# A graph-attention kernel's last layer: the barrier between projection and attention taken out, and its first attention step made beside the last projection rounds

## The chip, the cores and the metric

The kernel runs on one core of a Trainium2 chip. The metric is the device time of one execution in microseconds (us); the median of three runs of the kernel before is 1928.7 us (1923.83 to 1929.61). Everything below that has a moment in it ("at 1560.74") counts from the start of the profiled execution's span.

## The reference, cut to what matters

Two graph networks follow each other on 1250 nodes with 768 features and 40000 edges. The change is in the last convolution of the second one (in the kernel: layer DD), a relational graph attention with three edge types and one head:

```python
h = jax.nn.elu(h)                       # output of the convolution before
xr = jnp.einsum('nd,rdf->rnf', h, W)    # three projections, 768 x 768 each
alpha = jax.nn.leaky_relu((xr[etype, dst] @ q) + (xr[etype, src] @ k), 0.2)
m = segment_max(alpha, dst);  e = jnp.exp(alpha - m[dst])
z = segment_sum(e, dst);      a = e / (z[dst] + EPS)
out = segment_sum(a[:, :, None] * xr[etype, src], dst) + b
x = _layernorm(x + out)
```

## The kernel before, in words

**Dense form.** Nodes are padded to 1280, ten tiles of 128. Edges are counted into dense tables (`counts`, one per edge type), so attention is a dense product: for every pair of a source tile and a target tile, weights `counts * exp(...)` times projected rows. The last layer does both its projection and its attention with seven block products in place of eight (a Strassen scheme of 2 x 2 blocks: the names P1 to P7 and the sums `s1`..`s4`, `t1`..`t4`).

**Projection** (`project_d` on each engine). Six units (three types, two column halves) of five tile pairs make 30 rounds (`ROUNDS`). In a round TensorE (PE) makes seven products of 192 columns into PSUM (L1202), ScalarE (ACT) copies three of them (`keep_a`, `keep_b`, `keep_c`, L1563) and a fourth block (`fetch_c21`, L1585), VectorE (DVE) adds the rest up (`c22` L2096, `c11` L2087, `c12` L2109 to L2112), and ACT stores the round's five blocks to HBM (`store`, L1592, tensor `hs_d`). The products of two rounds are interleaved by the list `ORDER_D`; the semaphore `d_prod` counts them, and `DONE_D` is the count at which a given one is done. The last product of all is P3 of round 29. In between, DVE has searched the maxima, and from round 25 on the shift rows `pq` are turned, stored and fetched back to all partitions (`pq_rows_d`, L631, semaphore `pq_in`).

**Barrier.** Then every engine calls `end_phase`, which drains it and waits until all five have arrived. ACT comes to it only when all stores have landed:

```python
                store(ROUNDS - 1)
                for i in range(BLOCKS):
                    act.wait_ge(*d_blk_out[i].at(16 * ring_share(ROUNDS, i, BLOCKS)))
```

**Attention.** 75 steps: five groups `g` of two target tiles, and in each 15 pairs `m` of an edge type and a pair of source tiles. For step n, SyncE's queue (SP) loads projected rows `hs_d` (`h_load`, L796, 960 KB) into one of four places `h_slot`; DVE makes four quarters of exponents (`exponents_d`, L2367, in two instructions), ACT raises them (`exp_d`, L1788, two), DVE multiplies by the counts (`weights_d`, L2375, two) and makes six block sums (`sums_d`, L2385 to L2394; the fourth of them, L2390, is the first to read the loaded rows); PE multiplies (L1366, seven products of 384 or 385 columns). `d_ready` counts steps prepared, `d_used` steps multiplied. A load into a place, and exponents into one of four `a_slot`, wait until the step four before has been multiplied. The exponents of step n + 1 come ahead of the weights of step n.

All places of the attention (`a_slot`, `h_slot`) lie in `work`, over operands of the projection (`xT`, `xs`, `wsum`), and so can be written only when the projection is over. The order on SP after the barrier is load 0, load 1, the `pq` rows of type 1 (two transfers of 640 KB), loads 2, 3 and 4, the `pq` rows of type 2, loads 5 and on.

Of the kernel before, what the change touches and what calls it, by code (L numbers as in the profile page):

```python
# [29 lines left out]
P = 128  # L30
# [115 lines left out]
S_ROUND, MAX_ROUND, PQ_ROUND = 6, 8, 25  # L146
SAVE_AT = 1
# [9 lines left out]
def gnn_program(nc, t_in, out):  # L157
    with ExitStack() as ctx:
# [414 lines left out]
        def _(sp):  # L573
# [60 lines left out]
            def project_d(ci, s, ph):  # L634
# [26 lines left out]
                end_phase(sp, ph)  # L661

            def layer(ci, c, ph):
# [29 lines left out]
                if c is DD:  # L693
                    project_d(ci, s, ph)
# [96 lines left out]
                else:  # L791
                    def h_load(n):
# [3 lines left out]
                        sp.dma_start(h_slot[n % H_SLOTS][:, 0:5, 0:FH],  # L796
# [39 lines left out]
        def _(pool):  # L836
# [45 lines left out]
            for k in range(2, 6):  # L882
                end_phase(pool, k)
# [5 lines left out]
        def _(pe):  # L889
# [342 lines left out]
            def layer(ci, c, ph):  # L1232
# [74 lines left out]
                if c is DD:  # L1307
                    project_d(ci, s)
                    end_phase(pe, ph)
# [12 lines left out]
                pe.wait_ge(ones, 1 if c is A else ci)  # L1322
                if c is not DD:
                    body = c.unroll * c.R
# [23 lines left out]
                else:  # L1348

                    for g in range(TH):  # L1350
                        for m in range(STEPS_D):
                            n = g * STEPS_D + m
                            pe.wait_ge(d_ready, n + 1)
                            a, h = a_slot[n % A_SLOTS], h_slot[n % H_SLOTS]
                            for i, name in enumerate(PRODUCTS):
# [10 lines left out]
                                last = mm(bank(product_bank(g, i), width), a[:, at * P:(at + 1) * P], h[:, block_, 0:width],  # L1366
# [20 lines left out]
        def _(act):  # L1387
# [150 lines left out]

            def project_d(ci, s):
# [67 lines left out]
                for q in range(ROUNDS + 1):  # L1607
# [26 lines left out]
                    if q >= TH and q % TH == 0 and q // TH + 1 < len(UNITS):  # L1634
                        act.wait_ge(d_prod, DONE_D[q - 1, "P3"])
                        w_load(q // TH + 1)
                store(ROUNDS - 1)
                for i in range(BLOCKS):
                    act.wait_ge(*d_blk_out[i].at(16 * ring_share(ROUNDS, i, BLOCKS)))

            def layer(ci, c, ph):
# [122 lines left out]
                if c is DD:  # L1764
                    project_d(ci, s)
                    end_phase(act, ph)
# [11 lines left out]
                else:  # L1778
# [4 lines left out]
                    def exp_d(n):  # L1783
                        r, p = PAIRS_D[n % STEPS_D]
                        for q in range(2):
# [740 lines left out]
```

## Time and profile before

| what | value |
|---|---|
| median of 3 runs | 1928.7 us (1923.83 to 1929.61) |
| the profiled execution: its time, its span | 1925.18 us, 1923.3 us |
| granted TensorE clock, mean of the span | 0.973 |
| PE busy | 1777.4 us (92%) |
| DVE busy | 1549.1 us (81%) |
| ACT busy | 727.3 us (38%) |
| attention products of the last layer (L1366) | 341.1 us busy, 11.1 us idle before them |
| projection products of the last layer (L1202, the group that the page shows) | 98.1 us busy, 2.2 us idle before them |
| exponentials of the last attention (L1788) | 150 of them, 68.0 us busy, mean 500 ns |

Read it so: PE is the busiest engine over the span, but that is an average over stages. The idle time ahead of a line says how long the engine stood still just before instructions of that line, and what released it. Matmuls are pipelined and their ends are modelled, so their durations overlap; the distance between starts is the better measure of pace.

### The profile page before, as it was taken

The numbers are of one execution on the slowest core, as the hardware profiler recorded it, in microseconds if no ns is written. First come the engines' busy times: TensorE is split into PE (matmuls) and PEld (weight loads), VectorE is DVE, ScalarE is ACT, GpSimd is POOL, SyncE is SP. The second block draws the span as 40 slices with busy tenths as digits, with TensorE's granted clock in tenths as the row PEclk, the third lists the DMA queues.
The fourth block names the chain that finished last, engine by engine and source line by source line (L and its number), as shares of the span: only waits on it lengthen the run. The fifth ranks groups of instructions, "written<-read, shape, count | busy, mean of one in ns | idle before, by whom it ended". The sixth has DMA issues, their size and how long they took to land. (4 is left out here: it accounts for less than half of the span.)

```text
span 1923.3 us, 24256 instructions
## 1 busy us (share of the span) xinstructions
PE 1777.4 (92%) x8426; PEld 1334.4 (69%) x8427; DVE 1549.1 (81%) x2948; ACT 727.3 (38%) x1247; POOL 19.1 (1%) x40
## 2 busy tenths in 40 slices
PE   4789977599999899999999999997999979999997
PEld 3534545499854455555899999997899965555554
DVE  7799868999568554999999999996457547998896
ACT  4878966543224221111444434442311212332331
POOL 0000001000000000000000000000000000000000
PEclk8989989799999899999999999998999989999999
DMA  6200149441350327766412121211366457767764
GB/s 183 68 14 26 52 149 401 142 136 54 97 188 17 144 80 225 251 229 199 136 59 84 59 82 61 70 47 31 96 210 200 158 208 244 253 220 247 257 209 166
DMA packets 168068, 276.66 MB, mean 144 GB/s; under 512 B 11819, under 2 KB 132386, under 8 KB 164486
## 3 DMA queue, kind: packets, MB, share of 16 engines
q1 hardware_dynamic: 114342, 211.25, 33.7%
q10 hardware_dynamic: 50336, 49.66, 8.0%
q0 software_dynamic: 3264, 14.16, 1.9%
q8 instruction: 69, 1.13, 0.2%
q14 instruction: 57, 0.47, 0.1%
HBM read 219.31 MB, written 55.71 MB: 143 GB/s over the span
## 5 line engine op out<-in xcount | busy, mean ns | idle before, releaser
L1366 PE MATMUL ps<-work 128*128 128x384 f32 (+1 forms) x1050 | 341.1, 488 | 11.1 <-DVE work L2394 11.1
L1366 PEld LDWEIGHTS ps<-work 128*128 128x128 f32 x1050 | 199.7, 190 | 152.2 <-issue 12.9
L1293 PE MATMUL ps<-work 128*128 128x384 f32 (+1 forms) x720 | 237.0, 490 | 3.4 <-ACT work L1656 2.6
L1343 PE MATMUL ps<-counts,work 128*128 128x193 f32 x1440 | 239.3, 327 | 0.1
L1343 PEld LDWEIGHTS ps<-counts,work 128*128 128x128 f32 x1440 | 235.9, 190 | 0.4 <-DVE work L2266 0.4
L1750 ACT ACTIVATE work<-work,s 128x1280 f32<-128x1280 f32 x112 | 152.6, 1363 | 210.0 <-DVE work L2260 210.0
L1293 PEld LDWEIGHTS ps<-work 128*128 128x128 f32 x720 | 136.3, 190 | 100.8 <-issue 15.3
L2266 DVE SCALAR_TENSOR_TENSOR work<-work,counts 128x1280 f32<-128x1280 f32 x112 | 166.3, 1485 | 1.4 <-ACT work L1750 1.3
L1343 PE MATMUL ps<-counts 128*128 128x193 f32 x960 | 160.8, 327 | 1.4 <-POOLq L536 1.4
L1343 PEld LDWEIGHTS ps<-counts 128*128 128x128 f32 x960 | 157.4, 190 | 2.0 <-POOLq L536 2.0
L1918 DVE TENSOR_SCALAR work<-work,winoff 125x480 bf16<-125x480 f16 x480 | 157.8, 397 | 0.4 <-issue 0.3
L1788 ACT ACTIVATE work<-work,s 128x256 f32<-128x256 f32 x150 | 68.0, 500 | 222.5 <-DVE work L2367 222.4
L1343 PE MATMUL ps<-work 128*128 128x198 f32 x800 | 136.1, 334 | 15.3 <-DVE work L2266 15.3
L1343 PEld LDWEIGHTS ps<-work 128*128 128x128 f32 x800 | 135.6, 192 | 15.8 <-issue 15.7
L1018 PE MATMUL ps<-work 125*128 125x480 bf16 x480 | 113.0, 384 | 30.0 <-DVE work L1918 17.8
L2260 DVE SCALAR_TENSOR_TENSOR work<-work,sd 128x1280 f32<-128x1280 f32 x76 | 117.4, 1546 | 7.4 <-PE ps L1343 7.4
L1018 PEld LDWEIGHTS ps<-work 125*128 125x128 bf16 x480 | 46.9, 101 | 91.8 <-issue 44.0
L1451 ACT ACTIVATE work<-work 125x128 f16<-125x128 f16 x320 | 102.1, 394 | 11.1 <-issue 9.0
L1202 PE MATMUL ps<-work 128*128 128x192 f32 (+1 forms) x540 | 98.1, 329 | 2.2 <-DVE work L2109 1.5
L1750 ACT ACTIVATE counts<-counts,s 128x1280 f32<-128x1280 f32 x48 | 65.5, 1364 | 80.1 <-DVE counts L2260 79.2
L1202 PEld LDWEIGHTS ps<-work 128*128 128x128 f32 x540 | 89.9, 191 | 3.5 <-issue 2.3
L1726 ACT ACTIVATE work<-ps 128x384 f32<-128x384 f32 x60 | 29.5, 492 | 165.4 <-PE ps L1293 165.4
(278 smaller groups left out, 2428.5 us busy)
## 6 DMA issues: line engine op xcount, KB each, us to landing
work<-hs_d SPq DMA_DIRECT2D x75, 960.0 KB, 5.4
work<-nomask_d SPq DMA_DIRECT2D x70, 320.0 KB, 3.2
work<-pqrow_d SPq DMA_DIRECT2D x12, 1280.0 KB, 6.3
nomask_d<-work SPq DMA_DIRECT2D x40, 320.0 KB, 7.0
hx_d<-work ACTq DMA_DIRECT2D x60, 192.0 KB, 2.2
counts<-hx_d SPq DMA_DIRECT2D x120, 96.0 KB, 1.9
hs_d<-feat ACTq DMA_DIRECT2D x22, 480.0 KB, 3.6
counts<-pqrow_d SPq DMA_DIRECT2D x6, 1280.0 KB, 6.4
```

What stands on the lines that cost most here:

```text
L1018: return mm(bank(b, WROW), oh_lo[slot][0:EC, :], oh_hi[slot][0:EC, :], start=start, stop=False, skip_group_check=True)
L1202: last = mm(bank(at, n_), left[:, j, :], right[:, j, 0:n_], start=(start and j == 0), stop=(j == 2), skip_group_check=True)
L1293: last = mm(bank(n % 4 if i else n % 2, cols), xT[:, j, t * P:(t + 1) * P], wv[:, j, :], start=(j == 0), stop=(j == DT - 1))
L1343: last = mm(sums_at(c, t, u), xe_of(c)[i % RING][:, t * P:(t + 1) * P], hx[:, i % RING, 0:1 + c.width], start=(r == 0 and k == 0 and t % T ...
L1366: last = mm(bank(product_bank(g, i), width), a[:, at * P:(at + 1) * P], h[:, block_, 0:width], start=(m == 0), stop=(m == STEPS_D - 1), sk ...
L1451: last = nc.scalar.activation(lo_abs[0:EC, q * P:(q + 1) * P], iota_lo[0:EC, :], ACT.Abs, bias=nlof[0:EC, bass.ds(c0 + q, 1)])
L1726: nc.scalar.activation(stage[n % 3][:, 0:c.piece], bank(b, c.piece), ACT.Copy).then_inc(s.proj_ev.sem, 1)
L1750: nc.scalar.activation(w_, w_, ACT.Exp, bias=s02[:, k, bass.ds(rh, 1)], scale=0.8).then_inc(s.exp_done.sem, 1)
L1788: nc.scalar.activation(w_, w_, ACT.Exp, bias=s02[:, p + q * TH, r:r + 1], scale=0.8).then_inc(d_exp, 1)
L1918: return v.tensor_scalar(oh_hi[slot][0:EC, :], iota_hi[0:EC, :], winoff[0:EC, bass.ds(w, 1)], keyf[0:EC, bass.ds(ch, 1)], ALU.add, ALU.is_ ...
L2260: v.scalar_tensor_tensor(xe_of(c)[i % RING][:, 0:n_], p_, sd[:, k, bass.ds(rh, 1)], q_, ALU.add, ALU.max).then_inc(s.x_ready.sem, 1)
L2266: v.scalar_tensor_tensor(w_, w_, 3.0e38, counts[:, rel, k, lo:lo + n_], ALU.min, ALU.mult).then_inc(s.p_ready.sem, 1)
```

## The change

The barrier after the last layer's projection (phase 5) is gone on all five engines, and what it ordered is now ordered by single waits.

- The first attention step gets places of its own: `a_slot[0]` lies in the table `total`, and place 0 of the projected rows lies where the weight operand `raw[0]` was (last used by round 24), its seventh block behind the first place of `blocks`. The other three places of each stay in `work`.
- SP issues load 0 as soon as round 24 is done and the rows' own stores have landed; load 1 waits for the last product of the projection (`d_prod` at `len(ORDER_D)`); the `pq` rows of type 2 wait for all stores. Loads of the first 15 steps wait for the two stores that made their rows.
- DVE makes the exponents of step 0 at the end of round 27, its weights after round 28 and its sums after round 29's turn of the loop (`FIRST_STEP_D`); ACT raises the exponents in round 28's turn.
- PE waits before step 0 for the last PSUM readers (`d_c21`, `d_c12`), and before step 1 for the column of ones.

Its core (the moved functions `exponents_d`, `weights_d` and `sums_d` are unchanged but for `h_slot`, which became `h_block`, and are left out):

```diff
-        a_slot = [carve(work, i * 1024, 1024) for i in range(A_SLOTS)]
-        h_at = A_SLOTS * 1024
-        h_slot = [carve(work, h_at + i * 7 * H_PITCH, 7 * H_PITCH) for i in range(H_SLOTS)]
-        h_slot = [v.rearrange("p (b c) -> p b c", b=7) for v in h_slot]
-        h_ones = carve(work, h_at, H_SLOTS * 7 * H_PITCH).rearrange("p (s b c) -> p s b c", s=H_SLOTS, b=7)[:, :, 0:3, FH:FH + 1]
-        t_at = h_at + H_SLOTS * 7 * H_PITCH
+
+
+        a_slot = [total[:, NP:NP + 1024], *(carve(work, i * 1024, 1024) for i in range(A_SLOTS - 1))]
+        h_at = (A_SLOTS - 1) * 1024
+        h_later = [carve(work, h_at + i * 7 * H_PITCH, 7 * H_PITCH).rearrange("p (b c) -> p b c", b=7) for i in range(H_SLOTS - 1)]
+        h_first = carve(work, raw_at, 6 * H_PITCH).rearrange("p (b c) -> p b c", b=6)
+        h_first_t4 = total[:, blk_at + 5 * QH:blk_at + 5 * QH + FH]
+        assert 6 * H_PITCH <= RAW and NP + 1024 <= 2 * NP and 2 * NP + 4 * D <= blk_at + 5 * QH
+
+        def h_block(n, i, width=FH):
+
+            slot = n % H_SLOTS
+            if slot:
+                return h_later[slot - 1][:, i, 0:width]
+            return h_first[:, i, 0:width] if i < 6 else h_first_t4[:, 0:width]
+
+        def h_loaded(n):
+
+            return (h_later[n % H_SLOTS - 1] if n % H_SLOTS else h_first)[:, 0:5, 0:FH]
+
+        ones_first = h_first[:, 0:3, FH:FH + 1]
+        ones_later = carve(work, h_at, (H_SLOTS - 1) * 7 * H_PITCH)
+        ones_later = ones_later.rearrange("p (s b c) -> p s b c", s=H_SLOTS - 1, b=7)[:, :, 0:3, FH:FH + 1]
+        t_at = h_at + (H_SLOTS - 1) * 7 * H_PITCH
...
                         m = n % STEPS_D
-                        sp.dma_start(h_slot[n % H_SLOTS][:, 0:5, 0:FH],
+                        if n < STEPS_D:
+
+                            for half in range(2):
+                                q = (2 * (m // TH) + half) * TH + m % TH
+                                sp.wait_ge(*d_blk_out[q % BLOCKS].at(16 * (q // BLOCKS + 1)))
+                        if n < 2:
+                            sp.wait_ge(d_prod, DONE_D[ROUNDS - 1 - TH, "P3"] if n == 0 else len(ORDER_D))
+                        sp.dma_start(h_loaded(n),
                                      hs_d[m * P:(m + 1) * P, :].rearrange("p (b c) -> p b c", b=5)).then_inc(d_h_in[n % H_SLOTS], 16)
...
-                            if g == 0 and m in (1, H_SLOTS):
-                                pq_rows_d(ci, s, 1 if m == 1 else 2)
+                            if g == 0 and m == 1:
+                                pq_rows_d(ci, s, 1)
+                            if g == 0 and m == H_SLOTS:
+
+                                for i in range(BLOCKS):
+                                    sp.wait_ge(*d_blk_out[i].at(16 * ring_share(ROUNDS, i, BLOCKS)))
+                                pq_rows_d(ci, s, 2)
...
-                            a, h = a_slot[n % A_SLOTS], h_slot[n % H_SLOTS]
+                            a = a_slot[n % A_SLOTS]
+                            if n == 0:
+
+                                pe.wait_ge(d_c21, ROUNDS)
+                                pe.wait_ge(d_c12, ROUNDS)
+                            if n == 1:
+                                pe.wait_ge(ones, ci)
...
+                    if q == FIRST_STEP_D + 1:
+                        exp_d(0)
                 store(ROUNDS - 1)
-                for i in range(BLOCKS):
-                    act.wait_ge(*d_blk_out[i].at(16 * ring_share(ROUNDS, i, BLOCKS)))
...
+                    if q == FIRST_STEP_D:
+                        exponents_d(s, 0)
+                    if q == FIRST_STEP_D + 1:
+                        weights_d(0)
+                    if q == FIRST_STEP_D + 2:
+                        dve.wait_ge(d_prod, DONE_D[ROUNDS - 1 - TH, "P3"])
+                        mark(v.memset(ones_first, 1.0))
+                        sums_d(0, n_link[0])
...
-                end_phase(dve, ph)
+                if c is not DD:
+                    end_phase(dve, ph)
...
-                    v.memset(h_ones, 1.0).then_inc(ones, 1)
+                    dve.wait_ge(d_prod, len(ORDER_D))
+                    v.memset(ones_later, 1.0).then_inc(ones, 1)
...
-                    exponents_d(0)
+                    exponents_d(s, 1)
                     for n in range(total):
                         g, m = n // STEPS_D, n % STEPS_D
-                        if n + 1 < total:
-                            exponents_d(n + 1)
-                        sums_d(n, weights_d(n))
+                        if n and n + 1 < total:
+                            exponents_d(s, n + 1)
+                        if n:
+                            sums_d(n, weights_d(n))
```

How this moves instructions. On SP's queue before, from the fetch of the first `pq` rows (`pq_rows_d(ci, s, 0)`, the last two transfers ahead of the barrier) on:

```order
L631 DMA feat<-pqrow_d 128x1280 [waits pq_out]
L631 DMA counts<-pqrow_d 128x1280
L796 DMA work<-hs_d 128x5x384 [waits phase]
L796 DMA work<-hs_d 128x5x384
L631 DMA feat<-pqrow_d 128x1280 x2
L796 DMA work<-hs_d 128x5x384 x2
L796 DMA work<-hs_d 128x5x384 [waits d_used]
L631 DMA feat<-pqrow_d 128x1280 x2
L796 DMA work<-hs_d 128x5x384 [waits d_used] x5
```

and in the changed kernel (`layers_hx_out0` to `2` and `d_blk_out` are the semaphores of landed stores):

```order
L651 DMA feat<-pqrow_d 128x1280 [waits pq_out]
L651 DMA counts<-pqrow_d 128x1280
L822 DMA work<-hs_d 128x5x384 [waits d_prod,layers_hx_out1,layers_hx_out0]
L822 DMA work<-hs_d 128x5x384 [waits d_prod,layers_hx_out2,layers_hx_out1]
L651 DMA feat<-pqrow_d 128x1280 x2
L822 DMA work<-hs_d 128x5x384 [waits d_blk_out,layers_hx_out2]
L822 DMA work<-hs_d 128x5x384 [waits layers_hx_out0,d_blk_out]
L822 DMA work<-hs_d 128x5x384 [waits layers_hx_out1,layers_hx_out0,d_used]
L651 DMA feat<-pqrow_d 128x1280 [waits layers_hx_out2,d_blk_out,layers_hx_out1,layers_hx_out0]
L651 DMA feat<-pqrow_d 128x1280
L822 DMA work<-hs_d 128x5x384 [waits d_blk_out,layers_hx_out2,d_used]
```

The order of the transfers is the same; load 0 now waits for stores and `d_prod` and not for the phase, and so does each later load of the first group.

On DVE before, from the last but one `c12` (L2109) of the projection into the first attention step:

```order
L2109 TENSOR_TENSOR work<-ps,counts 128x192 [waits d_b,d_prod]
L2111 TENSOR_TENSOR counts<-work,counts 128x192 [waits d_c12]
L2112 TENSOR_TENSOR counts<-counts,work 128x192
L2096 TENSOR_TENSOR feat<-ps,counts 128x192 [waits d_c,d_prod]
L2109 TENSOR_TENSOR work<-ps,counts 128x192 [waits d_b,d_prod]
L2111 TENSOR_TENSOR feat<-work,feat 128x192 [waits d_c12]
L2112 TENSOR_TENSOR feat<-feat,work 128x192
L2289 MEMSET work 128x4x3 [waits phase]
L2367 SCALAR_TENSOR_TENSOR work<-feat,sd,counts 128x256 [waits layers_pq_in0,bias_in]
L2367 SCALAR_TENSOR_TENSOR work<-feat,sd,counts 128x256 x3
L2375 SCALAR_TENSOR_TENSOR work<-work,counts 128x256 [waits d_exp] x2
```

and in the changed kernel, from the same place on (L2182 to L2185 are `c12`, L2169 is `c22`, L2250 and L2373 set the ones, L2104 to L2113 are `sums_d`, L2086 is `exponents_d`, L2094 `weights_d`):

```order
L2182 TENSOR_TENSOR work<-ps,counts 128x192 [waits d_b,d_prod]
L2184 TENSOR_TENSOR counts<-work,counts 128x192 [waits d_c12]
L2185 TENSOR_TENSOR counts<-counts,work 128x192
L2250 MEMSET work 128x3 [waits d_prod]
L2104 TENSOR_TENSOR counts<-counts 128x128 [waits s_dve]
L2105 TENSOR_TENSOR counts<-counts 128x128
L2107 TENSOR_TENSOR counts<-counts 128x128 [waits s_dve]
L2109 TENSOR_TENSOR work<-work 128x384 [waits d_h_in0]
L2111 TENSOR_TENSOR counts<-counts 128x128 [waits s_dve]
L2113 TENSOR_TENSOR counts<-work 128x384 [waits s_dve]
L2169 TENSOR_TENSOR feat<-ps,counts 128x192 [waits d_c,d_prod]
L2182 TENSOR_TENSOR work<-ps,counts 128x192 [waits d_b,d_prod]
```

The six sums of step 0 now stand between the `c12` of round 28 and the `c22` of round 29; the exponents and weights of step 0 stand in the same way behind the `c12` of rounds 26 and 27.

## Rows read from the trace of the kernel before

**Rows 1.** The chain that ended last, in order of time: start us, us, what.
```profile
1561.83 3.17 DMA hs_d<-feat
...
1571.86 339.86 PE ps L1366 x1046
```

**Rows 2.** Timeline of PE: start us, us, engine, line, operation, count, [idle before, releaser].
```profile
1559.60 1.14 PE L1202 MATMUL ps<-feat,work 128*128 128x192 f32 x6
1571.86 8.47 PE L1366 MATMUL ps<-work 128*128 128x385 f32 x20 [11.13 <-DVE work L2394]
```

**Rows 3.** Timeline of DVE, end of the projection.
```profile
1545.14 0.36 DVE L2096 TENSOR_TENSOR feat<-ps,counts 128x192 f32<-128x192 f32 x1 [2.40 <-ACT counts L1563]
...
1558.57 0.36 DVE L2096 TENSOR_TENSOR feat<-ps,counts 128x192 f32<-128x192 f32 x1 [2.17 <-ACT counts L1563]
1560.77 0.36 DVE L2109 TENSOR_TENSOR work<-ps,counts 128x192 f32<-128x192 f32 x1 [1.85 <-PE ps L1202]
```

**Rows 4.** SP's queue: start us, us, line, what, count.
```profile
1529.44 0.43 SPq L631 DMA_DIRECT2D counts<-pqrow_d  x1
1565.10 1.26 SPq L796 DMA_DIRECT2D work<-hs_d  x2
...
1567.78 11.17 SPq L796 DMA_DIRECT2D work<-hs_d  x3
...
1582.95 18.61 SPq L796 DMA_DIRECT2D work<-hs_d  x5
```

**Rows 5.** Timeline of DVE, first attention steps.
```profile
1570.49 0.56 DVE L2390 TENSOR_TENSOR work<-work 128x384 f32<-128x384 f32 x1 [2.22 <-DMA work<-hs_d]
...
1572.42 0.75 DVE L2375 SCALAR_TENSOR_TENSOR work<-work,counts 128x256 f32<-128x256 f32 x2
1573.21 0.29 DVE L2385 TENSOR_TENSOR work<-work 128x128 f32<-128x128 f32 x1
...
1574.96 0.87 DVE L2367 SCALAR_TENSOR_TENSOR work<-feat,sd,counts 128x256 f32<-128x256 f32 x2
...
1579.34 0.56 DVE L2390 TENSOR_TENSOR work<-work 128x384 f32<-128x384 f32 x1 [2.11 <-DMA work<-hs_d]
...
1587.48 0.88 DVE L2367 SCALAR_TENSOR_TENSOR work<-feat,sd 128x256 f32<-128x256 f32 x2 [0.25 <-PE ps L1366]
...
1592.00 0.88 DVE L2367 SCALAR_TENSOR_TENSOR work<-feat,sd 128x256 f32<-128x256 f32 x2 [0.41 <-PE ps L1366]
```

**Rows 6.** Stretches: length; busy us (x) of PE, PEld, DVE, ACT, POOL; PEclk, DMA share, GB/s.
```profile
1561.83:1565.10 3.27, 0.00 (x0) 0.00 (x0) 0.00 (x0) 0.00 (x0) 0.00 (x0) 1.00 0.71 225
1565.10:1566.50 1.40, 0.00 (x0) 0.00 (x0) 1.35 (x5) 0.72 (x2) 0.00 (x0) 0.54 0.10 10
1565.10:1579.32 14.22, 7.46 (x18) 4.36 (x19) 9.76 (x30) 3.52 (x8) 0.00 (x0) 0.64 0.93 325
1565.10:1590.35 25.25, 18.49 (x52) 10.85 (x53) 19.83 (x60) 6.25 (x14) 0.00 (x0) 0.80 0.98 347
```

**Rows 7.** The first two attention steps: PE busy, PEld busy, PEclk, DMA share, GB/s.
```profile
1571.86:1582.87 11.01, 11.01 (x29) 6.42 (x30) 0.84 1.04 376
```

**Rows 8.** DMA issues: KB each, us to landing (the page; then 1520 to 1600).
```profile
work<-hs_d SPq DMA_DIRECT2D x75, 960.0 KB, 5.4
...
counts<-pqrow_d SPq DMA_DIRECT2D x1, 640.0 KB, 5.7
```

**Rows 9.** Timeline of ACT, round 28.
```profile
1549.58 0.33 ACT L1563 ACTIVATE counts<-ps 128x192 f32<-128x192 f32 x1 [2.65 <-DVE feat L2112]
1550.58 0.33 ACT L1563 ACTIVATE counts<-ps 128x192 f32<-128x192 f32 x1 [0.67 <-PE ps L1202]
1551.54 0.33 ACT L1563 ACTIVATE counts<-ps 128x192 f32<-128x192 f32 x1 [0.62 <-PE ps L1202]
```

**Rows 10.** PE after a short gap early in the span, and the stretch behind it.
```profile
331.35 0.73 PE L1078 MATMUL ps<-identb,work 128*128 128x128 bf16 x10 [2.82 <-DVE work L1990]
...
333.23:336.64 3.41, 3.41 (x27) 1.82 (x22) 3.41 (x5) 0.94 (x3) 0.00 (x0) 0.53 0.91 357
```

More of the change, by code:

```diff
@@ L881, in _ @@
             nc.gpsimd.memset(wub[0:1, :, D:D + 1], 1.0).then_inc(wub_zero, 1)
-            for k in range(2, 6):
+            for k in range(2, 5):
                 end_phase(pool, k)
@@ L1537, in _, with exp_d @@
             end_phase(act, 0)
+            def exp_d(n):
+                r, p = PAIRS_D[n % STEPS_D]
+                for q in range(2):
+                    act.wait_ge(d_x, 2 * n + q + 1)
+                    w_ = a_slot[n % A_SLOTS][:, q * 256:(q + 1) * 256]
+                    nc.scalar.activation(w_, w_, ACT.Exp, bias=s02[:, p + q * TH, r:r + 1], scale=0.8).then_inc(d_exp, 1)
             def project_d(ci, s):
@@ L1781, in f_norm @@
                         nc.scalar.activation(sdev[:, 0, t:t + 1], mv[:, t, 1:2], ACT.Sqrt, bias=epsc[:, 0:1]).then_inc(n_sqrt, 1)
-                    def exp_d(n):
-                        r, p = PAIRS_D[n % STEPS_D]
-                        for q in range(2):
-                            act.wait_ge(d_x, 2 * n + q + 1)
-                            w_ = a_slot[n % A_SLOTS][:, q * 256:(q + 1) * 256]
-                            nc.scalar.activation(w_, w_, ACT.Exp, bias=s02[:, p + q * TH, r:r + 1], scale=0.8).then_inc(d_exp, 1)
                     def copy_p1(g):
@@ L2040, in mark, with exponents_d, weights_d, sums_d @@
                 return n_link[0]
+            def exponents_d(s, n):
+                g, (r, p) = n // STEPS_D, PAIRS_D[n % STEPS_D]
+                if n >= A_SLOTS:
+                    dve.wait_ge(d_used, n - A_SLOTS + 1)
+                if n < STEPS_D and p == 0:
+                    dve.wait_ge(*s.pq_in[r % 2].at(32 * (r // 2 + 1)))
+                for q in range(2):
+                    w_ = a_slot[n % A_SLOTS][:, q * 256:(q + 1) * 256].rearrange("p (a c) -> p a c", a=2)
+                    v.scalar_tensor_tensor(w_, target_pair(pq_all[r][0], g), sd[:, p + q * TH, r:r + 1],
+                                           target_pair(pq_all[r][1], g), ALU.add, ALU.max).then_inc(d_x, 1)
+            def weights_d(n):
+                g, (r, p) = n // STEPS_D, PAIRS_D[n % STEPS_D]
+                for q in range(2):
+                    dve.wait_ge(d_exp, 2 * n + q + 1)
+                    w_ = a_slot[n % A_SLOTS][:, q * 256:(q + 1) * 256].rearrange("p (a c) -> p a c", a=2)
+                    made = mark(v.scalar_tensor_tensor(w_, w_, 3.0e38, target_pair(counts[:, r, p + q * TH, :], g),
+                                                       ALU.min, ALU.mult))
+                return made
+            def sums_d(n, made):
+                a11, a21, a12, a22, s1, s2, s3, s4 = (a_slot[n % A_SLOTS][:, i * P:(i + 1) * P] for i in range(8))
+                b11, b21, t1, b22, t3, t2, t4 = (h_block(n, i) for i in range(7))
+                dve.wait_ge(s_dve, made)
+                m1 = mark(v.tensor_tensor(s1, a21, a22, ALU.add))
+                v.tensor_tensor(s3, a11, a21, ALU.subtract)
+                dve.wait_ge(s_dve, m1)
+                m2 = mark(v.tensor_tensor(s2, s1, a11, ALU.subtract))
+                dve.wait_ge(d_h_in[n % H_SLOTS], 16 * (n // H_SLOTS + 1))
+                m3 = mark(v.tensor_tensor(t2, b22, t1, ALU.subtract))
+                dve.wait_ge(s_dve, m2)
+                v.tensor_tensor(s4, a12, s2, ALU.subtract)
+                dve.wait_ge(s_dve, m3)
+                v.tensor_tensor(t4, t2, b21, ALU.subtract).then_inc(d_ready, 1)
             def project_d(ci, s, rows_of_maxima):
```

47 lines of the change are left out of this document (7 added, 40 removed).

## Prediction, made before the changed kernel was run

> **What bounds the kernel now.** I read the chain that ended last first, since PE's 92% is an average over stages. In the stretch that the change touches the chain shows three things: a store of projected rows that takes 3.17 us to land, and behind it a run of attention products that goes on from 1571.86 for 339.86 us without a break [rows 1]. So from its first attention step on PE is the bound, and whatever brings that step forward, and lets the next ones follow closely, comes off the end one for one. PE's timeline gives the size of the hole ahead of it: the last projection products end at 1559.60 + 1.14 = 1560.74, the first attention product starts at 1571.86, and PE stands still for 11.13 us [rows 2].
>
> What fills the hole: DVE makes the last `c12` at 1560.77, for 0.36 us [rows 3]; ACT starts the last store at 1561.83; it lands at 1565.00 [rows 1]; that, and no engine's work, is what the barrier waits for. SP then starts load 0 at 1565.10 [rows 4]; DVE takes the loaded rows at 1570.49 after waiting 2.22 us for them [rows 5], 1571.86 - 1570.49 = 1.37 us before PE begins.
>
> **A second cost hides in the hole.** The granted clock was 1.00 while the last store was landing and 0.54 on average just after, from 1565.10 [rows 6]. That is the lower level, 1.2 GHz, which PE gets having stood still for 4.4 us. PE's first two attention steps therefore took 11.01 us, until 1582.87, at a mean clock of 0.84 [rows 7]. I put their end at 1582.87 because SP starts load 5, which waits for them, at 1582.95 [rows 4]. A step at full clock takes 1592.00 - 1587.48 = 4.52 us, the distance of two exponent instructions that each wait for a step's products [rows 5]; I use 4.53, which also fits step 2's end (1582.87 + 4.53 = 1587.40). Two steps at full clock would have taken 9.06, so the low clock cost 11.01 - 9.06 = 1.95 us.
>
> **The change, part by part.** The number to find is when step 2 starts: 1582.87 before. From there on both kernels do the same.
>
> *Step 0.* It no longer waits for a load on the critical path. Load 0 now goes out behind the first `pq` rows. The second of these was started at 1529.44 and took 5.7 us [rows 4, 8], so they are there at 1535.1; even a whole load of 5.4 us [rows 8] behind that is there by about 1541, 15 us before it is read. What DVE adds to the last rounds:
> - two exponents, 0.88 us [rows 5], behind the `c12` of round 26. DVE stood idle for 2.40 us ahead of the `c22` at 1545.14 [rows 3], and the `pq` rows have been there for 7 us: hidden.
> - two weights, 0.75 us [rows 5], one round (6.83 us) later, in the same gap of 2.40. They wait for ACT's two exponentials. These stand behind the copy at 1549.58, which ends at 1549.91, and end at about 1550.9 (two at the page's mean of 500 ns); ACT's next copy was due at 1550.58 and moves by some 0.3 us, its next one at 1551.54 had 0.62 us of idle time ahead of it [rows 9], and takes this up. The second weight ends at about 1551.4, before the `c22` of 1551.97. Hidden.
> - a memset and six sums in the gap of 2.17 us ahead of the last `c22` at 1558.57 [rows 3]. The sums from L2385 on take 1.75 us (L2385 at 1573.21, the next step's exponents at 1574.96 [rows 5]), with the memset some 1.85, and they can start when the `c12` of round 28 is done, at 1556.4: done at 1558.3. Hidden, with 0.3 us to spare. If that cover were gone, `c22` would have 0.67 us more, as it ended at 1558.93 and P3, which it releases, began at 1559.60 [rows 2].
>
> Then PE waits for the last `c12`, which ends at 1561.13 (it frees a PSUM bank), and starts step 0 some 0.15 us later: 1561.3. It ends at 1565.8.
>
> *Steps 1 and 2.* Their places still lie over the projection's operands, so loads 1 and 2 can't leave before 1560.8, and here the transfers set the pace. Before, from 1565.10 on, SP sent load 0, load 1, two `pq` rows and load 2: 3 x 960 + 2 x 640 KB = 4.26 MB. Load 2 was there at 1579.34, 14.22 us later, at a mean of 325 GB/s [rows 4, 5, 6]. The first 1.40 us moved almost nothing (10 GB/s) [rows 6]; the other 12.82 us give 3.0 us for each MB. Now load 0 is gone from that queue, but the last store (128 x 5 x 192 x 4 bytes = 480 KB), started at 1561.83, runs beside it: 2 x 960 + 2 x 640 + 480 KB = 3.77 MB. So 1.4 + 12.82 x 3.77 / 4.26 = 12.75 us, and load 2 is there at 1573.55. With the 1.37 us of sums behind a load, step 2 starts at **1574.9**.
>
> Does load 1 come later than that allows? Load 0 before took 5.36 us with load 1 behind it; with the store's 0.49 MB beside it up to 1.5 us more, so it is there between 1566.2 and 1567.7. Step 1 then runs from 1567.5 to 1569.0 at the start, to 1572.1 to 1573.6 at the end, ahead of 1574.9. DVE's own work for step 1 up to its load (memset, four exponents, two weights, three sums from 1561.8) is done by 1565.3. So PE has two short gaps, 1.7 to 3.2 us ahead of step 1, and 1.3 to 2.8 ahead of step 2, and load 2 alone sets the result.
>
> *Later loads.* SP used to stop at load 4 until step 0 was multiplied; that step now ends at 1565.8, before its turn comes. Load 4, the `pq` rows of type 2 and load 5 queue up behind one another. Before, load 5 was there at 1590.35, after 25.25 us and 5.90 + 2.62 = 8.52 MB at 347 GB/s [rows 6]; now 8.03 MB, so 1.4 + 23.85 x 8.03 / 8.52 = 23.9 us: 1584.7. Step 5 starts at 1574.9 + 3 x 4.53 = 1588.5 and needs it at 1587.1. It is 2.4 us early; loads 3 and 4 (3 us each, at 1576.5 and 1579.5) are early too, and DVE, which needs 3.3 us for a step, keeps up.
>
> *Sum.* 1582.87 - 1574.9 = 8.0 us gained. In other terms: of 11.13 + 1.95 = 13.08 us, 0.5 stay as the wait for `c12` and 4.5 as the two gaps. The span goes from 1923.3 to 1915.3 and the profiled execution from 1925.18 to 1917.2. That execution is 3.5 us under the median of the runs shown, for which I take the same difference: 1928.7 - 8.0 = **1920.7 us**.
>
> *Bounds of the unknown.* No row shows a load beside a store. If the store costs the loads nothing, 3.28 MB take 11.3 us, step 2 starts at 1573.5 and the gain is 9.4. If load 2 takes 14.22 us as before, step 2 starts at 1576.4 and the gain is 6.5. I take the proportional value, since the DMA share was 0.93 to 0.98 in both long stretches [rows 6], that is, they were full. The Trainium skill (DMA: Bandwidth & Descriptors, "Issuing engines are not separate DMA queues") says that transfers started from different engines run on the same 16 DMA engines and interleave; by that rule the store is paid for in full, and the gain is 8.0 and not 9.4.
>
> **The rivals.**
>
> *The clock falls in the short gaps.* Early in the span PE stood still for 2.82 us only, went on at 331.35, and the clock was at 0.53 for the 3.41 us from 333.23 [rows 10]: a gap shorter than the one at hand can bring the lower level. If it falls for step 1, that step is up to 1.95 us longer and mostly still ends before load 2 is ready. If it falls for step 2, nothing hides it: gain 8.0 - 1.95 = 6.0, 1922.7 us. Against it: the gaps are shorter than the 4.4 us ahead of the fall before, with a whole step at full pace between them, and after a slow step 1 the second gap nearly closes. The Trainium skill (TensorE: Matmul & The Clock Gate, "HAM oscillation") describes this case, bursts of products with waits for data between them, where the clock drops in each wait and each burst starts slow; by it this rival would be the rule.
>
> *Loads slower than their share.* The store goes ahead of load 2 in full and load 2 takes its 14.22 us as well: 15.7 us, step 2 at 1577.9, gain 5.0, 1923.7 us. It speaks for it that the read and the written side may disturb each other, against it that the DMA engines were full before too.
>
> *The transfers don't hold.* If both loads came in time, PE would wait for `c12` alone: step 2 at 1561.3 + 9.06 = 1570.4, gain 12.5, 1916.2 us. This needs load 2 after 8.2 us, 3.28 MB at over 400 GB/s with no start-up.
>
> *The change doesn't do what it says,* as the inserted work isn't hidden. All of it on PE's path is 0.88 + 0.75 + 1.85 + 1.0 = 4.5 us, gain 3.5, 1925.2 us. The gaps on DVE speak against it.
>
> *Slower than before.* Load 5 comes too late: with SP no longer held at load 4, the queue depends on the rate alone. At the 225 GB/s that the stretch of the last store moved [rows 6], 8.03 MB take 35.7 + 1.4 us, load 5 is there at 1597.9, step 5 starts at 1599.3, and not at 1582.87 + 3 x 4.53 = 1596.5 as before: 2.8 us lost, 1931.5 us. It decides from below some 245 GB/s (load 5 at 1595.1). The 347 GB/s of before for the same mixture speak against it.
>
> **How the numbers follow.** Forecast 50% (gain 6.5 to 9.4); clock in step 2 22%; slower loads 10%; loads in time 6%; work not hidden 7%; late load 5, or some other loss, 5%. Two executions of one kernel differ by 5.8 us in the runs shown, and about 0.3% (5.8 us) is what a measurement can tell from no change. Over 0.3% faster is the forecast, the loads in time, and 14 of the 22% of the clock, whose 6.0 us lies at the edge; within 0.3% the rest of that, slower loads, work not hidden, and 1 of the last case's 5. That makes 0.70, 0.26 and 0.04. The range runs from the loads in time (1916.2) to the work not hidden (1925.2), about 1 us wider at either end for the median's own scatter: 1915 to 1926.
>
> **What the profile of the changed kernel would show.** PE: first attention product at 1561.3, then a gap of 1.7 to 3.2 us that the rows of load 1 end, a gap of 1.3 to 2.8 us that those of load 2 end, and none at steps 3 to 5. Rounds 27 to 29 without new idle time on PE. The granted clock at 1.00 over all of it, or 0.5 in step 1. DVE waiting for `hs_d` rows at steps 1 and 2 alone. The last `c22` within 0.3 us of where it was. I am wrong if a gap stands ahead of step 5, if the clock is low in step 2 or later, or if the two gaps add up to more than 6 us.

## The result and the profile after

| | kernel before | changed kernel |
|---|---|---|
| median, us (7 runs each) | 1928.7 (1923.83 to 1932.97) | 1921.99 (1917.05 to 1924.24) |
| ratio to before | 1 | 0.9969, 95% interval 0.9955 to 0.9983 |
| profiled execution: time, span | 1925.18, 1923.3 | 1923.26, 1921.4 |
| granted clock, mean of the span | 0.973 | 0.971 |

The ratio is a gain of 6.0 us (3.3 to 8.7). 8.0 was forecast, and 1920.7 us. A second measurement of the changed kernel, among the experiments, gave 0.9961 (0.9947 to 0.9976), 7.5 us. By itself the 6.0 us can't tell the forecast from its rival of the clock in step 2, which had put the gain at just 6.0 and the time at 1922.7 us. The trace has to do that.

The two profiled executions differ by only 1.9 us. So I look at the place of the change first, and at the rest afterwards. A common clock is needed for that, because the two are not at the same point of the program at the same moment. I count from **c**, the start of the last `c12` on DVE: 1560.77 before [rows 3], 1565.94 after.

PE of the changed kernel, from its first attention product on (timeline; L1402 was L1366):

```profile
1566.45 4.12 PE L1402 MATMUL ps<-work,counts 128*128 128x385 f32 x12 [0.54 <-DVE work L2182]
...
1573.57 4.79 PE L1402 MATMUL ps<-work 128*128 128x385 f32 x14 [2.36 <-DVE work L2113]
...
1580.72 9.31 PE L1402 MATMUL ps<-work 128*128 128x385 f32 x28 [2.36 <-DVE work L2113]
```

The one hole of 11.13 us [rows 2] has become three: 0.54 us for the last `c12`, and 2.36 us ahead of step 1 and ahead of step 2. Step 2 starts at c + 14.78. Before, the prediction had it at c + 22.10 (1582.87), just ahead of SP's next load at 1582.95. But [rows 7] count 29 products in the stretch up to there, where two steps are 28. The timeline of the kernel before shows the 29th, the first of step 2, start at 1582.76:

```profile
1582.76 0.48 PE L1366 MATMUL ps<-work 128*128 128x385 f32 x1
```

That is c + 21.99, so 7.2 us are gained here. Nearly all of it arrives at the end: the last attention product starts at c + 351.7 before (1912.5) and at c + 344.7 after (1910.6), 7.0 or 7.1 us earlier. In the same way all starts of step 2 below are the starts of its first product.

What ends the two gaps stands on DVE (L2182 is `c12`, L2169 is `c22`, L2094 `weights_d`, L2109 the first sum that reads loaded rows):

```profile
1555.51 0.82 DVE L2094 SCALAR_TENSOR_TENSOR counts<-counts 128x256 f32<-128x256 f32 x2 [0.77 <-ACT counts L1580]
1557.13 0.36 DVE L2169 TENSOR_TENSOR counts<-ps,counts 128x192 f32<-128x192 f32 x1 [0.80 <-ACT counts L1606]
...
1563.73 0.36 DVE L2169 TENSOR_TENSOR feat<-ps,counts 128x192 f32<-128x192 f32 x1 [0.28 <-ACT counts L1606]
1565.94 0.36 DVE L2182 TENSOR_TENSOR work<-ps,counts 128x192 f32<-128x192 f32 x1 [1.85 <-PE ps L1233]
...
1572.28 0.56 DVE L2109 TENSOR_TENSOR work<-work 128x384 f32<-128x384 f32 x1 [2.33 <-DMA work<-hs_d]
...
1579.43 0.56 DVE L2109 TENSOR_TENSOR work<-work 128x384 f32<-128x384 f32 x1 [3.72 <-DMA work<-hs_d]
...
1590.55 0.56 DVE L2109 TENSOR_TENSOR work<-work 128x384 f32<-128x384 f32 x1 [1.04 <-DMA work<-hs_d]
```

The work put into the last rounds is hidden: DVE still waits 0.80 and 0.28 us ahead of its `c22`, and the last `c22` is 2.21 us ahead of the last `c12`, where it was 2.20 before [rows 3]. Step 1 and step 2 wait for transfers. The chain that ended last says the same of step 2, and names the queue ahead of the load:

```profile
1565.99 0.52 SPq L822
...
1566.56 0.78 SPq L651
...
1567.39 0.47 SPq L651
...
1567.96 11.45 DMA work<-hs_d
```

Load 1 leaves at c + 0.05, the two transfers of `pq` rows stand behind it, and load 2 needs 11.45 us from its own start. In stretches (length, busy us of the five engines, PEclk, DMA share, GB/s), from the start of load 1 to the landing of load 2, and then steps 0 and 1:

```profile
1565.99:1579.43 13.44, 9.55 (x28) 5.15 (x28) 7.29 (x24) 2.61 (x6) 0.00 (x0) 1.00 1.01 339
1566.45:1580.72 14.27, 9.55 (x29) 5.12 (x29) 8.15 (x26) 2.61 (x6) 0.00 (x0) 1.00 1.03 351
```

The DMA engines are full (share 1.01), and the granted clock is 1.00 throughout. The low clock cost 10.90 - 9.04 = 1.9 us before (two steps from 1571.86 to 1582.76, against 4.52 us each at full clock). They are not paid here.

**Where the rest of the 7.2 us is in the profiled execution.** c itself comes 5.17 us later than before. That was lost long ahead of the change, in code that it doesn't touch: at the start of the third layer PE has two waits (timeline of PE and a stretch, kernel before)

```profile
1329.87 1.51 PE L1150 MATMUL ps<-identf,feat 128*128 128x128 f32 x6 [8.02 <-DVE feat L2051]
...
1344.86 0.88 PE L1150 MATMUL ps<-identf,feat 128*128 128x128 f32 x6 [0.90 <-DVE feat L2051]
```
```profile
1320.00:1350.00 30.00, 17.71 (x101) 15.95 (x100) 21.49 (x49) 10.80 (x17) 0.00 (x0) 0.83 0.13 40
```

and the same in the changed kernel:

```profile
1332.90 1.51 PE L1181 MATMUL ps<-identf,feat 128*128 128x128 f32 x6 [8.02 <-DVE feat L2124]
...
1349.86 0.88 PE L1181 MATMUL ps<-identf,feat 128*128 128x128 f32 x6 [0.36 <-DVE feat L2124]
```
```profile
1320.00:1350.00 30.00, 18.37 (x85) 16.80 (x85) 19.04 (x43) 8.86 (x13) 0.00 (x0) 0.72 0.13 40
```

3.03 us are lost by the first row, so still further ahead (where, I haven't followed), and 5.00 by the second. The remaining 1.97 us are lost between the two rows. The clock was low behind the 8.02 us of waiting in both, but for longer in the second (0.72 against 0.83 over these 30 us). Executions of one kernel spread over 6 to 10 us; a single pair of profiles can't show a gain of this size at the end of the span, a place in it can.

### The profile page after: what moved, and what is told of

Its sections match the earlier page's. It is cut to its first block, busy times and chain, and to the rows that moved or that the text cites. A ratio compares the mean times of both kernels' runs of the same rounds, so it can differ in the third digit from the quotient of the medians.

```text
span 1921.4 us, 24266 instructions
## 1 busy us (share of the span) xinstructions
PE 1782.4 (93%) x8426; PEld 1338.4 (70%) x8427; DVE 1549.6 (81%) x2949; ACT 727.2 (38%) x1247; POOL 19.1 (1%) x40
## 4 chain that ended last, share of the span: by engine, by line
PE 47%; DVE 2%; DMA 1%; ACTq 0%; ACT 0%; issue 0%; DVEq 0%; SPq 0%
PE ps L1373 20%; PE ps L1402 17%; PE ps L1233 9%; DMA work<-hs_d 1%; ACTq L1588 0%; PE ps L1181 0%; DMA work<-in_w_d 0%; DVE feat L2124 0%; ACT work L1599 0%; DVE work L2342 0%; ACT counts L1606 0%; DVEq L556 0%; DVE counts L2194 0%; DVE work L2132 0%; DVE work L2135 0%
## 5 line engine op out<-in xcount | busy, mean ns | idle before, releaser
L1402 PE MATMUL ps<-work 128*128 128x384 f32 (+1 forms) x784 | 256.7, 486 | 4.7 <-DVE work L2113 4.7
L1324 PE MATMUL ps<-work 128*128 128x384 f32 (+1 forms) x720 | 238.8, 493 | 4.5 <-ACT work L1699 2.6
L1402 PEld LDWEIGHTS ps<-work 128*128 128x128 f32 x784 | 148.7, 190 | 109.9 <-DVE work L2113 5.9
L1324 PEld LDWEIGHTS ps<-work 128*128 128x128 f32 x720 | 137.4, 191 | 102.5 <-issue 17.0
L1373 PEld LDWEIGHTS ps<-work 128*128 128x128 f32 x800 | 135.6, 192 | 15.8 <-issue 15.7
L1580 ACT ACTIVATE work<-work,s 128x256 f32<-128x256 f32 x112 | 50.7, 500 | 162.0 <-DVE work L2086 161.9
L1233 PEld LDWEIGHTS ps<-work 128*128 128x128 f32 x540 | 91.5, 194 | 3.5 <-issue 2.3
```

The lines of the kernel that those rows point to most:

```text
L1233: last = mm(bank(at, n_), left[:, j, :], right[:, j, 0:n_], start=(start and j == 0), stop=(j == 2), skip_group_check=True)
L1324: last = mm(bank(n % 4 if i else n % 2, cols), xT[:, j, t * P:(t + 1) * P], wv[:, j, :], start=(j == 0), stop=(j == DT - 1))
L1373: last = mm(sums_at(c, t, u), xe_of(c)[i % RING][:, t * P:(t + 1) * P], hx[:, i % RING, 0:1 + c.width], start=(r == 0 and k == 0 and t % T ...
L1580: nc.scalar.activation(w_, w_, ACT.Exp, bias=s02[:, p + q * TH, r:r + 1], scale=0.8).then_inc(d_exp, 1)
```

## The experiments

All are edits of the changed kernel. All are read at the place of the change, and timed where a ratio is given. The kernel before ran beside each of them on the same chip.

**The changed kernel again.** No edit.

> The changed kernel itself, once more, beside the others on the same chip. Theory: c varies by some us with the clock upstream, but step 1 starts at c + 7.6 and step 2 at c + 14.8 again, each within 0.3, and the ratio to the kernel before is 0.9962 (7.3 us of 1928). Rival (the local gain was one favourable execution, the clock falls in its two gaps in others): step 2 at c + 16.7, granted clock 0.5 in a part of steps 1 and 2.

Ratio 0.9961 (0.9947 to 0.9976). With c at 1561.41, step 1 starts at c + 7.58 and step 2 at c + 14.81. PE, and a stretch in step 1:

```profile
1568.99 6.48 PE L1402 MATMUL ps<-work 128*128 128x385 f32 x14 [2.32 <-DVE work L2113]
1576.22 4.47 PE L1402 MATMUL ps<-work 128*128 128x385 f32 x13 [0.75 <-DVE work L2113]
```
```profile
1570.30:1573.70 3.40, 3.40 (x7) 1.77 (x6) 0.80 (x4) 0.00 (x0) 0.00 (x0) 0.51 1.04 386
```

Here the clock did fall in step 1, which took 6.48 us where the first profile has 4.79, and the second gap shrank from 2.36 to 0.75 us. Step 2 starts where it did. The theory holds for the two starts, and the rival has a part: the fall happens in step 1, but it costs nothing, as load 2 is what step 2 waits for.

**The early step taken out, the barrier left out.**

```diff
-                            sp.wait_ge(d_prod, DONE_D[ROUNDS - 1 - TH, "P3"] if n == 0 else len(ORDER_D))
+                            sp.wait_ge(d_prod, len(ORDER_D))
...
-                    if q == FIRST_STEP_D:
-                        exponents_d(s, 0)
...
-                    exponents_d(s, 1)
+                    exponents_d(s, 0)
```

> The changed kernel without its early first step: exponents, weights and sums of step 0 and load 0 wait for the end of the projection like the others; the barrier stays out. Times are counted from the start of the last c12 on VectorE (c): kernel before, step 0 at c + 11.1 and step 2 at c + 22.1 us; changed kernel, step 0 at c + 0.5, step 1 at c + 7.6, step 2 at c + 14.8. Theory (the transfers that can only leave at c set the start, and two causes share the gain): load 0 lands some 6.3 us after c, step 0 starts at c + 7.7; TensorE has then stood still for over 7 us, longer than the 4.4 us after which the clock fell before, so the first steps lose up to 1.95 us again and step 2 starts at c + 18.7 (c + 17.8 if the clock stays up). The gain to the kernel before is 3.4 to 4.3 us, against 7.3 for the changed kernel. Rival (the barrier alone was the cost, the early step is hidden anyway): step 2 at c + 14.8, the gain stays 7.3.

Ratio 0.9988 (0.9975 to 1.0002). PE, with c at 1560.70; then a stretch from step 0's start; then SP, where the second row begins with load 5, which waits for the end of step 1:

```profile
1568.28 6.11 PE L1402 MATMUL ps<-work,counts 128*128 128x385 f32 x12 [7.62 <-DVE counts L2110]
```
```profile
1568.28:1572.00 3.72, 3.72 (x6) 2.18 (x7) 3.52 (x11) 0.91 (x2) 0.00 (x0) 0.50 1.06 414
```
```profile
1575.75 0.98 SPq L651 DMA_DIRECT2D feat<-pqrow_d  x2
1579.59 9.56 SPq L822 DMA_DIRECT2D work<-hs_d  x3
```

Step 0 starts at c + 7.58, at half clock (0.50), and step 2 at c + 18.69: a gain of 3.3 us at this place. The theory holds, the rival falls: without the early step less than half of the gain is there. The ratio alone can't tell this run from the kernel before, as its interval includes 1.

**The early step left in, the barrier put back.**

```diff
+                end_phase(sp, 5)
...
-            for k in range(2, 5):
+            for k in range(2, 6):
...
                 store(ROUNDS - 1)
+                for i in range(BLOCKS):
+                    act.wait_ge(*d_blk_out[i].at(16 * ring_share(ROUNDS, i, BLOCKS)))
+                end_phase(act, 5)
```

> The changed kernel with the barrier of phase 5 put back on all engines; step 0 is still made beside the last rounds and load 0 goes out ahead of the barrier. Theory: step 0 starts when the barrier opens, at c + 4.5, just as the clock falls, and takes up to 6.5 us; load 1 leaves at c + 4.3 and step 1 starts at c + 11.1; load 2, with 3.28 MB from c + 4.3 on, lands at c + 15.6 to c + 16.3, and step 2 starts at c + 17.0 to c + 17.7: a gain of 4.4 to 5.1 us to the kernel before. Rival (the barrier is the whole cost): no gain, step 2 at c + 22.

Ratio 0.9972 (0.9959 to 0.9984). PE, with c at 1563.74:

```profile
1568.11 7.12 PE L1410 MATMUL ps<-work,counts 128*128 128x385 f32 x12 [4.41 <-ACTq L556]
...
1581.31 9.31 PE L1410 MATMUL ps<-work 128*128 128x385 f32 x28 [0.92 <-DVE work L2124]
```

SP's load 1, DVE's first sum that reads load 2, and the stretch between them:

```profile
1568.08 0.52 SPq L828 DMA_DIRECT2D work<-hs_d  x1
```
```profile
1580.02 0.56 DVE L2120 TENSOR_TENSOR work<-work 128x384 f32<-128x384 f32 x1 [3.25 <-DMA work<-hs_d]
```
```profile
1568.08:1580.02 11.94, 11.91 (x28) 6.65 (x28) 6.42 (x20) 2.61 (x6) 0.00 (x0) 0.75 0.87 301
```

Step 0 starts at c + 4.37, when ACT (L556, the barrier) releases it, and step 2 at c + 17.57: a gain of 4.4 us. The last store had landed 0.14 us before PE's release (1564.79 + 3.18 = 1567.97 in the chain). So each part alone gives 3.3 or 4.4 and both 7.2. They need not add up exactly, since what step 2 waits for isn't the same: without the early step it is the end of step 1 (load 2's rows were taken 2.95 us before), with it, load 2.

**The `pq` rows of type 1 behind load 3.**

```diff
-                            if g == 0 and m == 1:
+                            if g == 0 and m == 3:
                                 pq_rows_d(ci, s, 1)
```

> The changed kernel with the two transfers of pq rows of type 1 (640 KB each) moved on the queue from behind load 1 to behind load 3. Theory (what the queue has to move ahead of load 2 sets step 2): load 2 has 2.46 MB ahead of and in it, the last store included, instead of 3.77 MB, and lands at c + 9 to c + 9.5 instead of c + 13.5; step 2 then starts when step 1 is done, at c + 11.6 to c + 12.2, without a gap, 2.6 to 3.2 us earlier than in the changed kernel (gain to the kernel before about 10). Rival (a fixed time per load, or the issuing queue, sets the gap): step 2 stays at c + 14.8.

Ratio 0.9949 (0.9929 to 0.9968). PE and DVE, with c at 1563.80:

```profile
1570.84 13.84 PE L1402 MATMUL ps<-work 128*128 128x385 f32 x42 [1.77 <-DVE work L2113]
```
```profile
1569.55 0.56 DVE L2109 TENSOR_TENSOR work<-work 128x384 f32<-128x384 f32 x1 [1.75 <-DMA work<-hs_d]
...
1573.42 0.56 DVE L2109 TENSOR_TENSOR work<-work 128x384 f32<-128x384 f32 x1 [0.44 <-DMA work<-hs_d]
...
1579.49 0.88 DVE L2086 SCALAR_TENSOR_TENSOR work<-feat,sd 128x256 f32<-128x256 f32 x2 [1.52 <-DMA feat<-pqrow_d]
```

Load 2 lands at c + 9.62 and not at c + 13.49, and three steps (42 instructions) follow without a gap from c + 7.04. Step 2 starts at 1575.47, c + 11.67, 3.1 us earlier than in the changed kernel. What moved are 1.31 MB that nobody needs before step 5, and there they now come 1.52 us late for DVE, which nearly had that to spare: PE loses 0.2 us there. The rival falls. The gain over the changed kernel is read from the place; the ratio's interval overlaps that of the changed kernel's second measurement (0.9947 to 0.9976).

**The `pq` rows of type 1 ahead of load 1.**

```diff
+                            if g == 0 and m == 1:
+                                sp.wait_ge(d_prod, len(ORDER_D))
+                                pq_rows_d(ci, s, 1)
                             h_load(g * STEPS_D + m)
```

> The changed kernel with the pq rows of type 1 ahead of load 1, to lengthen the gap between step 0 and step 1 on purpose. Theory: load 1 lands at c + 10.5, step 1 starts at c + 11.9, after TensorE has stood still for 6.8 us; this is longer than the 4.4 us after which the clock fell in the kernel before, so the granted clock goes to 0.5 and steps 1 and 2 lose up to 1.95 us: step 2 at c + 18.4. Rival (between two steps at full pace the clock stays up, whatever the gap): step 2 at c + 16.4 with the granted clock at 1.00.

One run. PE with c at 1564.68; then the gap in two stretches and step 1 with what follows:

```profile
1577.30 16.57 PE L1403 MATMUL ps<-work 128*128 128x385 f32 x42 [7.35 <-DVE work L2114]
```
```profile
1569.72:1572.65 2.93, 0.23 (x1) 0.00 (x0) 0.00 (x0) 0.00 (x0) 0.00 (x0) 0.99 0.99 326
1572.65:1577.30 4.65, 0.00 (x0) 0.00 (x1) 1.28 (x4) 0.00 (x0) 0.00 (x0) 0.50 1.07 396
1577.30:1584.80 7.50, 7.50 (x15) 4.26 (x16) 6.54 (x20) 1.81 (x4) 0.00 (x0) 0.63 1.06 391
```

Step 1 starts at c + 12.62, the clock falls some 2.7 us into the gap, and load 5, which waits for step 1, leaves at c + 20.2. Step 2 starts at 1584.67, c + 19.99, 1.6 us later than expected. The mechanism is the expected one, but load 1 came 0.8 us later than expected, and the low clock cost 16.57 - 13.84 = 2.7 us over three steps, not 1.95. The order of these transfers alone takes the gain to the kernel before from 7.2 down to 2.0 us.

**The last store held back.**

```diff
-                store(ROUNDS - 1)
+                def last_store():
+                    store(ROUNDS - 1)
+                return last_store
...
                                 exp_d(g * STEPS_D + m)
+                            if g == 0 and m == 4:
+                                last_store()
```

> The changed kernel with the last store of the projection (480 KB) held back until ScalarE has done the exponentials of step 4, so that it isn't beside loads 1 and 2. Theory (what the 16 engines have to move counts, whichever queue it is on): 3.0 us for each MB, so load 2 lands 1.5 us earlier than in the changed kernel, at c + 12.0, and step 2 starts at c + 13.3; load 1 lands up to 0.9 us earlier, at c + 5.4. Rival (the store and the loads don't hold each other up): both land as before, c + 6.3 and c + 13.5, step 2 at c + 14.8.

One run. DVE with c at 1558.28, then PE, then SP:

```profile
1564.75 0.56 DVE L2113 TENSOR_TENSOR work<-work 128x384 f32<-128x384 f32 x1 [2.46 <-DMA work<-hs_d]
...
1570.74 0.56 DVE L2113 TENSOR_TENSOR work<-work 128x384 f32<-128x384 f32 x1 [2.58 <-DMA work<-hs_d]
...
1586.49 0.56 DVE L2113 TENSOR_TENSOR work<-work 128x384 f32<-128x384 f32 x1 [5.67 <-DMA work<-hs_d]
```
```profile
1566.04 15.53 PE L1402 MATMUL ps<-work 128*128 128x385 f32 x42 [2.48 <-DVE work L2117]
...
1587.78 10.93 PE L1402 MATMUL ps<-work 128*128 128x385 f32 x33 [1.69 <-DVE work L2117]
```
```profile
1577.19 0.81 SPq L651 DMA_DIRECT2D feat<-pqrow_d  x2
```

Load 1 lands at c + 6.47 as before (6.34), load 2 at c + 12.46, 1.03 us earlier. So the store costs load 2 about 1.0 us (1.5 by the theory) and load 1 nothing, where the theory had up to 0.9: half right. This is one profile of one run against two of the changed kernel, whose own landings of load 2 (c + 13.49 and c + 13.53) are 0.04 us apart. The clock fell in step 1 (three steps took 15.53 us instead of 13.84), and with load 2 earlier this is no longer covered whole: step 2 can't start before 7.76 + 4.53 + 1.69 = c + 13.98, where its rows are ready at 13.83; it starts at c + 14.08. And it shows the rival of the late load 5 at work: the `pq` rows of type 2 wait for all stores, leave at c + 18.9 and not at c + 12.5, load 5 behind them lands at c + 28.2, and PE waits 1.69 us ahead of step 5. So the store held back brings step 2 forward by 0.7 us, and more than that is lost again by step 5.

**Load 1 in a place of its own.** With the `pq` rows of type 1 behind load 3 and those of type 2 behind load 6.

```diff
+        later_at = [XT_END, h_at, XT_END + 7 * H_PITCH]
+        h_later = [carve(work, at, 7 * H_PITCH).rearrange("p (b c) -> p b c", b=7) for at in later_at]
...
-                        if n < 2:
-                            sp.wait_ge(d_prod, DONE_D[ROUNDS - 1 - TH, "P3"] if n == 0 else len(ORDER_D))
+                        if n < 3:
+                            sp.wait_ge(d_prod, [DONE_D[ROUNDS - 1 - TH, "P3"], DONE_D[ROUNDS - 1, "P6"], len(ORDER_D)][n])
...
-                            if g == 0 and m == 1:
+                            if g == 0 and m == 3:
                                 pq_rows_d(ci, s, 1)
-                            if g == 0 and m == H_SLOTS:
+                            if g == 0 and m == 6:
```

> The changed kernel with three more changes: the pq rows of type 1 behind load 3; the rows of step 1 in a place over xs[0] and xs[1], which the last P6 frees, so that load 1 leaves when that product is done, 4.4 us ahead of c; the pq rows of type 2 behind load 6. Theory (load 1 and the queue ahead of load 2 are all that is left): load 1 has landed by c + 1.9, step 1 is held by VectorE alone, which needs until about c + 5.3 with its weights in the places of the projection, a gap of some 0.3 us; load 2 lands by c + 6.5, step 2 starts at c + 9.8: gain 12.3 us to the kernel before, 5.0 to the changed one, a ratio of about 0.9936 to the kernel before. Rival (VectorE becomes the bound when the loads are early): step 1 at c + 5.3 too, but each further step 3.3 us of VectorE plus waits behind, gaps again at steps 2 and 3, step 2 at c + 11 or later.

Median 1915.73 us (1914.83 to 1916.83) against 1928.05; ratio 0.9939 (0.9926 to 0.9952), 11.8 us. PE with c at 1563.45:

```profile
1563.95 4.12 PE L1403 MATMUL ps<-work,counts 128*128 128x385 f32 x12 [0.54 <-DVE work L2183]
...
1568.67 13.84 PE L1403 MATMUL ps<-work 128*128 128x385 f32 x42
...
1582.35 4.04 PE L1403 MATMUL ps<-work,counts 128*128 128x385 f32 x12
```

Step 1 starts at c + 5.22, step 2 at 1573.30, c + 9.85: 12.1 us ahead of the kernel before, 4.9 ahead of the changed one, and step 4 follows at c + 18.90. Of 11.13 us of hole and 1.9 of low clock some 0.9 are left, 0.54 of them the wait for `c12`. The rival falls: DVE is done with step 2's sums before PE is done with step 1.

## Why the prediction was right, point by point

- **The hole and what fills it.** Right. The barrier waited for the store: with it put back PE is released by ACT at c + 4.37, 0.14 us after the store has landed. The part of the low clock is right too: the next step is slow in all four traces in which PE stood still here for 4.4 us or more (0.50 in step 0 without the early step). The sum has it at 1.95 us, measured are 1.9.
- **Step 0.** Forecast c + 0.53, measured c + 0.51. All three insertions into the last rounds were hidden, the tightest with 0.28 us to spare (forecast 0.3).
- **Step 1.** Forecast c + 6.7 to c + 8.2, measured c + 7.63 and 7.58.
- **Step 2,** the number that sets the result. The mechanism was right, as moving 1.31 MB on the queue moves step 2 by 3.1 us. The size was off: c + 14.13 forecast, c + 14.78 and 14.81 measured, 0.65 us late. With its start before at c + 21.99 and not c + 22.10, 7.2 us were gained and not 8.0. The term that was mis-sized is "1.4 + 12.82 x 3.77 / 4.26 = 12.75 us", which measured 13.44, and it was wrong in two ways.

  *The bytes.* It has one store beside the loads. There were two: the store of the round before is started 0.91 us ahead of c, and before, the barrier had kept it as well as the last one out of the loads' way. ACT's queue in the changed kernel, and what the two queues moved between the start of load 1 and the landing of load 2 (packets, MB, busy share; q1 is SP's, q10 ACT's):

```profile
1565.03 0.52 ACTq L1635 DMA_DIRECT2D hs_d<-counts  x1
1566.99 0.52 ACTq L1635 DMA_DIRECT2D hs_d<-feat  x1
```
```profile
q1 hardware_dynamic: 1794, 3.58, 77.3%
q10 hardware_dynamic: 1312, 0.98, 23.4%
```

  0.98 MB are two stores of 0.49.

  *The rate.* Load 1, the `pq` rows and load 2 are 3.28 MB in three of the traces, with no store beside them, one or two. They took 11.94 us with none (barrier put back), 12.41 with the first alone (last store held back), and 13.44 with both. So the 3.28 MB alone needed 0.7 us more than the 11.3 of the prediction's scaling, the store that wasn't counted cost 0.5 us, and the one that was cost 1.0 instead of 1.5. Each is one profile. The errors go in both directions and partly cancel: that step 2 came within 0.65 us of the forecast is in part luck.

  Against the MB counted as in the prediction, five times of load 2, from SP's start of the first load, are 9.57 us for 2.46, 12.41 for 3.28, 13.44 for 3.77, 14.22 for 4.26 and 15.69 for 4.75. A line through them is 3.6 us + 2.57 us for each MB (390 GB/s), each point within 0.5 us, and the 11.94 us fit it too. The scaling had too small a fixed part, and so promised too much for fewer bytes. A part of it is that a later load's bytes ride along: 3.58 MB passed SP's queue in the 13.44 us and not 3.28. The rest isn't settled.
- **The bounds.** The gain lies inside 6.5 to 9.4. The last store is paid for in part: 1.0 us for 480 KB. The Trainium skill (DMA: Bandwidth & Descriptors, "Issuing engines are not separate DMA queues") has transfers of all issuing engines interleave on the same 16 DMA engines, which speaks for a price. The traces agree in direction, at two thirds of the proportional price on load 2 and none on load 1.
- **The rival of the clock.** I had the clock's fall in step 1 as possible and hidden: it happened in the second profile of the changed kernel, and was hidden. The fall in step 2 was seen in none of the two profiles. The Trainium skill (TensorE: Matmul & The Clock Gate, "HAM oscillation") describes such falls in waits between bursts; the traces agree for gaps of 2.32 and 2.48 us, and differ for two of 2.36 and one of 1.77 us, after which the clock stayed at 1.00.
- **The late load 5.** Not in the changed kernel: it landed at c + 24.61 (forecast c + 23.9) and DVE waited 1.04 us for it, PE not at all. But the prediction had it follow load 4 and the `pq` rows of type 2 freely, and SP stood still ahead of those rows for 4.2 us, for the last store to land. Beside the loads this store took 11.4 us and not 3.17 [rows 1]:

```profile
SPq L847 <- DMA hs_d<-feat: 4.2, 1, 4.2
```
```profile
hs_d<-feat ACTq DMA_DIRECT2D x1, 480.0 KB, 11.4
```

  PE did wait for load 5 in the experiment that held back the store.
- **Whole program.** 1921.99 against 1920.7, inside the range; 6.0 and 7.5 us in two measurements, around the 7.2 of the place. The range says little: 1915 to 1926 also holds the medians of the variants with a half of the change (1925.01 and 1923.89) and of the best one (1915.73). And the ratios, 0.31% and 0.39% faster, are close to the 0.3% that the prediction took as its border to no change.

## What to carry to other kernels

When a barrier goes, look for what it leaves in front: here two transfers that only step 5 needed stood ahead of the rows of step 2, and moving them was worth 3.1 us, about as much as the barrier's removal alone (3.3). Count everything in flight there, as a barrier also keeps earlier stores out of the way of the loads behind it. Order the queue at such a seam by when each transfer is first needed, and look for an operand that dies a product or two before the end, since a load that left 4.4 us earlier closed the gap ahead of step 1 (1.77 us with the `pq` rows moved, none with this as well). A small change is best judged at its place, counted from an event that both kernels have; the ends of two profiled executions differed here by 1.9 us for a change worth 7.2.

## What the runs showed of the hardware that I had not expected

- **After nearly the same short gap the clock fell or stayed.** Gaps ahead of step 1 of 2.36, 2.32 and 2.48 us in nearly the same program left the clock at 1.00 once, and brought it to 0.5 within step 1 twice. What decides it isn't shown.
- **How long the clock stays down varies too,** for the same wait of 8.02 us at the start of the third layer: 0.83 on average over 30 us in one profile and 0.72 in the other, with 1.97 us lost between them. This is more than a quarter of what the change gives.
- **A store beside loads** cost load 2 1.0 us and load 1, which started just ahead of it, nothing. The store itself took 11.4 us to land beside them and 3.17 without them.
